# Wider rings and paired tail sums in the gather layers of a four-layer GNN kernel

## The reference

```python
edge_index = stack([src, dst])
# layer 0: tanh((segment_sum(sigmoid(att) * x[dst], src)) @ W0.T + b0)
# layer 1: h = where(deg > 0, segment_sum(x[src], dst), x);  h @ W1.T + b1
# layer 2: segment_sum(x[src] * edge_weight, dst)
# layer 3: segment_sum(x[src] * (edge_weight_n2 * edge_weight), dst)
x = layernorm(x + layer(x, ...))        # four times
```

## Time and profile before

| | |
|---|---|
| time, median of 3 runs | 11979.11 us (11966.0 to 11984.94) |
| the profiled execution's own time | 11878.79 us |
| its span | 11877.0 us |
| busy: PE, PEld, DVE, ACT, POOL | 8897.3, 5666.5, 7726.7, 5860.3, 8022.3 us |
| indirect gathers L801 | 5175, 4910.8 us busy |
| scatter stage and start | to 3946 us |
| gather layers 0, 1, 2 | 3946 to 6485, 6572 to 9178, 9228 to 11827 us |

### The profile page before, as it was taken

One profiled execution on the slowest core, in us unless ns is written; L12 is line 12 of the kernel. 1 busy time (PEld: TensorE's weight loads), 2 busy tenths in 40 slices (PEclk: granted clock), 3 DMA queues, 4 the chain that ended last, 5 costly groups with the idle time before them and its releaser, 6 DMA issues. The chain is left out here.

```text
span 11877.0 us, 171360 instructions
## 1 busy us (share of the span) xinstructions
PE 8897.3 (75%) x49605; PEld 5666.5 (48%) x49606; DVE 7726.7 (65%) x19171; ACT 5860.3 (49%) x13187; POOL 8022.3 (68%) x7169
## 2 busy tenths in 40 slices
PE   4787888888886455566666787888887788888887
PEld 2444444444444234444546455454445455554445
DVE  8777777777774655544444776666665776666665
ACT  4766555555553444333332665544443766544443
POOL 5787788888887566666665566666665566666665
PEclk8877777777776676767777899989988899889998
DMA  5433333334334211111111111111111111111111
GB/s 145 47 38 35 36 37 38 39 38 38 38 38 70 51 25 25 25 25 24 24 24 27 27 24 25 25 25 24 25 24 28 28 25 25 25 25 25 23 24 30
DMA packets 651932, 398.90 MB, mean 34 GB/s; under 512 B 456994, under 2 KB 563748, under 8 KB 649745
## 3 DMA queue, kind: packets, MB, share of 16 engines
q0 software_dynamic: 445920, 252.47, 17.5%
q1 hardware_dynamic: 201276, 132.08, 4.3%
q10 hardware_dynamic: 3814, 3.37, 0.1%
HBM read 283.23 MB, written 104.16 MB: 33 GB/s over the span
## 5 line engine op out<-in xcount | busy, mean ns | idle before, releaser
L801 POOL DMA_INDIRECT mem<-xt,mem x5175 | 4910.8, 949 | 2864.1 <-issue 1338.3
L1148 PE MATMUL ps<-mem 128*128 128x392 f32 (+5 forms) x6750 | 2905.2, 536 | 1079.8 <-DVE mem L1708 448.9
L722 POOL DMA_INDIRECT table<-mem,idx x1925 | 3000.4, 1559 | 746.4 <-issue 556.7
L1708 DVE TENSOR_TENSOR mem<-mem,ps 128x392 f32 (+3 forms) x3300 | 1917.4, 581 | 1966.8 <-remote 1007.5
L943 ACT ACTIVATE mem<-iota_f,mem 128x128 f32<-128x128 f32 x4200 | 1319.3, 390 | 2659.8 <-remote 1312.7
L1160 PE MATMUL ps<-mem,xs 128*64 128x94 f32 (+1 forms) x17640 | 2068.5, 271 | 382.5 <-issue 363.2
L1160 PEld LDWEIGHTS ps<-mem,xs 128*64 128x64 f32 (+1 forms) x17640 | 1803.8, 156 | 1026.7 <-issue 979.8
L1689 DVE TENSOR_SCALAR mem<-ps,mem 128x392 f32<-128x392 int16 (+5 forms) x4050 | 2175.9, 556 | 0.0
L1148 PEld LDWEIGHTS ps<-mem 128*128 128x128 f32 (+1 forms) x6750 | 1106.1, 184 | 1936.5 <-issue 1312.5
L922 ACT COPY mem<-zero_c 128x658 f32<-128x658 f32 x1260 | 895.6, 732 | 1370.5 <-remote 896.1
L1181 PE MATMUL ps<-mem 128*64 128x64 f32 (+1 forms) x10350 | 1031.7, 245 | 478.4 <-issue 456.2
(11 more groups left out here) (180 smaller groups left out, 7819.2 us busy)
## 6 DMA issues: line engine op xcount, KB each, us to landing
mem<-xt,mem POOLq DMA_INDIRECT x5175
mem<-key_rows SPq DMA_DIRECT2D x385, 160.0 KB
table<-mem,idx POOLq DMA_INDIRECT x1925
table<-mem POOLq DMA_DIRECT2D x3, 6304.0 KB
mem<-table SPq DMA_DIRECT2D x42, 448.0 KB, 5.2
xt<-xs SPq DMA_DIRECT2D x9, 896.0 KB
mem<-in_x_dram SPq DMA_DIRECT2D x415, 16.0 KB
w_d<-mem SPq DMA_DIRECT2D x2, 1562.5 KB, 7.8
```

The source lines that it names most:

```text
L722: pool.indirect_dma_start(out=tables[i % NTAB][:, :], out_offset=bass.IndirectOffsetOnAxis(ap=idx[:, i % (IDXS * GC):i % (IDXS * GC) + 1], ...
L801: pool.indirect_dma_start(out=gbuf[:, o:o + F], out_offset=None, in_=xt[l][:, :], in_offset=bass.IndirectOffsetOnAxis(ap=src_q[q % 2].bitc ...
L1148: last = pe.matmul(ps_d[b % PSD][:, 0:w], lo_l[:, r * P:(r + 1) * P], blk_l[:, r * DT:r * DT + w], start=(k == 0), stop=(k == parts - 1))
L1708: v.tensor_tensor(at, at, new, ALU.add).then_inc(d_add[l], 1)
```

## The change

The ring of gathered rows grows from six to eight slots, and the ring of tail one-hots from three to four. The product of a tail slot goes to one of four places in two PSUM banks, two slots to a bank. DVE no longer adds a slot's product in the next slot: in each odd slot n it adds those of n - 3 and n - 2, after one wait for both. PE waits for adds in even slots only. The tail one-hots are made one slot ahead and not two. The flush add comes one slot later than before (`ZONE_END[max(n - 1, 0)]` in place of `ZONE_END[n]`). The list pieces shrink to 100 chunks and 23 slots, which gives room for the rings; arrays behind them move up.

```diff
--- before.py
+++ after.py
@@ -54,8 +54,8 @@
 WC = 94
 FAR = 65536.0
 NOWHERE = 1048576.0
-R = 6
-OHR = 3
+R = 8
+OHR = 4
 BR = 10
 PSD = 4
 FZ = 14
@@ -165,7 +165,7 @@
     [max(0.17 * k * d, 0.12 * k * d + 0.14 * d + 0.2) for (_, k), d in zip(BLOCKS, ROWS_OF)], 1.5)
 
 
-QD, QT = 170, 45
+QD, QT = 100, 23
 NQD, NQT = -(-CD // QD), -(-NT // QT)
 
 
@@ -280,10 +280,10 @@
         GW = GC * XW
         gbuf = arena[:, 0:R * GW]
         OW = GC * WD
-        ohr = arena[:, 1950:1950 + OHR * OW]
-        blk = arena[:, 2910:2910 + BR * DT]
-        los = arena[:, 7810:7810 + BR * P]
-        lo_d = arena[:, 9090:9090 + GC * P]
+        ohr = arena[:, 2600:2600 + OHR * OW]
+        blk = arena[:, 3880:3880 + BR * DT]
+        los = arena[:, 8780:8780 + BR * P]
+        lo_d = arena[:, 10060:10060 + GC * P]
 
 
         own = [arena[:, 2910 + p * BT_ * XW:2910 + (p + 1) * BT_ * XW] for p in range(2)]
@@ -381,7 +381,7 @@
         ps_s = [ps[:, (5 + p) * BK:(6 + p) * BK] for p in range(2)]
         ps_d = [ps[:, k * BK:k * BK + DT] for k in range(PSD)]
         ps_d2 = [ps[:, 2 * p * BK:2 * (p + 1) * BK].rearrange("p (h c) -> p h c", h=2)[:, :, 0:DX // 2] for p in range(2)]
-        ps_w = [ps[:, (4 + p) * BK:(4 + p) * BK + WD] for p in range(2)]
+        ps_w = [ps[:, (4 + p) * BK + i * WD:(4 + p) * BK + (i + 1) * WD] for p in range(2) for i in range(2)]
         ps_f = ps[:, 6 * BK:6 * BK + WC]
         ps_x = ps[:, 6 * BK + 2 * P:6 * BK + 3 * P]
         iota_pairs = ps[:, 7 * BK:7 * BK + DT // 2].bitcast(I32)
@@ -1173,12 +1173,12 @@
                             zi += 1
                     pe.wait_ge(gath[n % R], gathered(l, n))
                     pe.wait_ge(oh_done[l], n + 1)
-                    if n >= 2:
-                        pe.wait_ge(acc_add[l], n - 1)
+                    if n >= 4 and n % 2 == 0:
+                        pe.wait_ge(acc_add[l], n - 2)
                     for k in range(GC):
                         o = (n % R) * GW + k * XW
                         q = (n % OHR) * OW + k * WD
-                        last = pe.matmul(ps_w[n % 2][0:M, :], gbuf[:, o:o + M], ohr[:, q:q + WD], start=(k == 0),
+                        last = pe.matmul(ps_w[n % 4][0:M, :], gbuf[:, o:o + M], ohr[:, q:q + WD], start=(k == 0),
                                          stop=(k == GC - 1), skip_group_check=True)
                     last.then_inc(agg_done[l], 1)
                 fixup(l, M)
@@ -1719,8 +1719,8 @@
                         v.wait_ge(acc_add[l], n)
                     if flushed:
                         v.wait_ge(f_add[l], flushed)
-                    v.wait_ge(agg_done[l], n + 1)
-                    v.tensor_tensor(at, at, ps_w[n % 2][0:M, :], ALU.add).then_inc(acc_add[l], 1)
+                    v.wait_ge(agg_done[l], min(n // 2 * 2 + 2, NT))
+                    v.tensor_tensor(at, at, ps_w[n % 4][0:M, :], ALU.add).then_inc(acc_add[l], 1)
 
                 def hots_up_to(b, added):
 
@@ -1731,27 +1731,29 @@
 
                 v.wait_ge(acc_zero, acc_cleared(l))
                 tail_hots(0)
-                tail_hots(1)
+                hot = hots_up_to(0, 0)
                 tail_weights(0)
-                hot = hots_up_to(0, 0)
-                tail_weights(1)
+                flushed = added = 0
                 for n in range(NT):
-                    if n:
-                        tail_add(n - 1, ZONE_END[n - 1] // FZ)
-                    if n + 2 < NT:
-                        tail_hots(n + 2)
+                    if n >= 3 and n % 2:
+                        for m in (n - 3, n - 2):
+                            tail_add(m, flushed)
+                        added = n - 1
+                    if n + 1 < NT:
+                        tail_hots(n + 1)
                     hot = hots_up_to(hot, BLOCK_END[n])
-                    if n + 2 < NT:
-                        tail_weights(n + 2)
-                    if n:
-                        for s_ in range(ZONE_END[n - 1] // FZ, ZONE_END[n] // FZ):
-                            flush_add(s_, n)
+                    if n + 1 < NT:
+                        tail_weights(n + 1)
+                    for s_ in range(flushed, ZONE_END[max(n - 1, 0)] // FZ):
+                        flush_add(s_, added)
+                        flushed += 1
                     for b in range(BLOCK_END[n], BLOCK_END[n + 1]):
                         block_add(b)
                         hot = hots_up_to(hot, b + 1)
-                for s_ in range(ZONE_END[NT - 1] // FZ, NSEG):
-                    flush_add(s_, NT - 1)
-                tail_add(NT - 1, NSEG)
+                for s_ in range(flushed, NSEG):
+                    flush_add(s_, added)
+                for n in range(added, NT):
+                    tail_add(n, NSEG)
                 v.wait_ge(acc_add[l], NT)
                 v.sem_inc(fix_free, 1)
                 fixup(l, M)
```

More of the change, by code:

```diff
@@ L365, in program @@
         nkt = key_f[:, 0:C0]
-        DENSE_AT = 9730
+        DENSE_AT = 10700
         dense = [mem[:, DENSE_AT + p * WC * T:DENSE_AT + (p + 1) * WC * T] for p in range(2)]
```

## The result

The changed kernel took 12043.39 us (median of 4, 12029.55 to 12050.64) where the kernel before took 11980.12 us (11966.0 to 11984.94): a ratio of 1.0059, 95% interval 1.0048 to 1.0071. It is slower by 63 us. The forecast was 11960 us, faster by 19 us; the time is inside the forecast range of 11720 to 12110 us, but on the other side of no change.

The account below looks back on a forecast made before the run. PE's signals were taken to be held back while POOL issues gathers, a beat of about 7.4 us a slot. Terms 0 - 19 - 6 + 10 = -15 us from 11979 gave 11964, stated as 11960 us; range 11720 to 12110.

Parts of the forecast that it names:

- the beat holds: Gather layers: the time per slot follows gathers issued and stays; 11960 us (11900 to 12010), chance 0.50.
- Eight slots: Ring of gathered rows: PE held off longer at layer starts, given back at layer ends; 0, bound +37.5 us.
- Longer runs: POOL's gathers: more runs two slots long between stops; at most 114 us, a sixth taken, -19 us.
- Tail adds: DVE's paired, later adds: the wait moves to block adds at L1708; -6 us, between 0 and -514 us.
- Flush add one slot later: Segment seams: PE's next segment may wait for DVE's later add; +10 us, between 0 and 244 us.
- the seams rival: PE stands at a segment's first zone for the late flush add; 122 us, 12100; chance 0.22, 0.20 of it slower.
- One-hots, smaller pieces: One-hots one slot ahead still come in time, and more list loads on SP delay nobody; 0 each.
- nothing comes faster: Steady part of a layer: POOL waits eight products back, but PE lies two slots further back; 0.

Follow-up runs that it names:

- free condition: Sessions in which the unchanged kernel before took 10666 to 10672 us; the changed kernel measured 0.9982 of it there.
- held condition: Sessions in which the unchanged kernel before took 11885 to 11980 us and POOL stopped in most slots; the changed kernel first measured 1.0059 of it there.
- the session with copies: Kernel before and changed kernel, each with SP copying two times 1 KB HBM to HBM per slot: 12016.37 and 12056.06 us; without copies the kernel before took 11968.72 us.
- four copies: Kernel before and changed kernel, each with SP copying four times 1 KB HBM to HBM per slot: 12093.66 and 12135.88 us.

## Why the prediction was wrong

The case that I forecast was that the beat holds, and where kernels can be compared at one level it did. The forecast said 19 us faster, 63 us slower was measured. The sum failed at the term for the ring; the gain from longer runs wasn't there; the term for the flush add was perhaps too small. From the sum's -15 us to +63 us are 78 us: 27 at the ring, 19 and 6 for two gains that weren't there, and 26 that stay open.

**Eight slots: 0, with +37.5 us as the bound.** This is the step that failed first. I wrote that the stop for the last zones "comes with one slot left and not three. That gives the two slots back: 0". The stop does come with one slot left, 5.97 us long like the 6.00 us of the earlier trace rows. But it gives little back, since what POOL waits for is not what ends the layer: PE has two more slots behind it, and the last zones too. The runs show +27 us for the ring alone, and the trace 6.8, 9.6 and 8.7 us of it at the ends of the three layers. That is 70% of the bound that I had worked out and set aside. In the free condition, where PE has no backlog, the cost is absent.

**Longer runs: -19 us.** Not there. In the session of the ring alone POOL's waits for PE come to 991.9 us ("remote") and 506.6 us (L1181), 1498.5 us in all, where the trace before has 995.1 + 487.0 = 1482.1 us. The ring adds slots to the first run only; the steady stops stay. The term rested on a stop that grows with the run before it, and the very rows that I used speak against that: in the earlier trace rows a single slot lies between 3994.52 and 4003.10 us, 8.58 us, and its stop is 2.63 us, longer than the 2.34 us after two slots. The first eight slots together take (4003.10 - 3946.82) / 8 = 7.04 us each and not the 6.81 us of the first seven. With the ring of eight the stop after one slot is even 6.15 us.

**Tail adds: -6 us, 0 to -514.** The wait moved to L1708 as written: 2707.9 us before L1708 in the changed kernel with the early flush add, against 1966.8, and its tail adds wait for about 180 us. POOL's waits for PE in that kernel are 926.1 + 559.5 = 1485.6 us, again as before. Adds in pairs and later one-hots together are worth nothing that these runs can tell: 1.0022 with them, 1.0024 without them, in two held sessions in which the kernel before is 6 us apart. The pairs with a ring of six never met the held condition.

**Flush add one slot later: +10 us, 0 to +244.** Perhaps too small; by how much, if at all, is not settled. What PE waited for ahead of the zones in the changed kernel has this line (us, times, longest):

```profile
PE ps L1160 <- DVE acc L1714: 55.4, 14, 6.8
```

With the flush add early it is gone; all that stands there is

```profile
  issue: 1329.8, 1969
  DVE mem L1708: 33.0, 39
  DVE mem L1669: 2.3, 2
  DVE mem L1689: 1.7, 3
```

and in the kernel with the ring alone there is no L1714 either. So the mechanism of the seams rival is in the trace; its price is not shown. In time, the whole change lost 63 us in one held session, and all of it but the late flush add lost 25 us in another, which leaves 38 us; by the session with copies it is 40 - 25 = 15 us. But the two losses of the whole change, 63 and 40 us, differ by 23 us themselves, and the changed kernel and its early form were never held in the same session. Against a high price stands the session with copies: there the changed kernel waits for flush adds just as long,

```profile
  DVE acc L1727: 57.7, 15
```

(L1727 is L1714), and what its span gains beyond PE's growing lag behind POOL is 31.6 - 22 = some 9 us, while POOL's waits are the same. (With four copies PE waits 27.5 us for flush adds, and the time lost is 42 us against 40.) So the late flush add costs somewhere between nearly nothing and 38 us, an unsettled part of the rival's 122 us. In the free session the two kernels were the same within 4 us: I take it that DVE's add there comes in time because no signal that DVE waits for is late.

**One-hots, smaller pieces: 0.** Pieces and places: 0.9997 in the free condition. Alone they were not timed in the held one; there they are part of the ring's +27 us.

So of the 63 us the ring carries some 27 and pairs and one-hots nothing that shows; the other 36 us stay open between the late flush add and what one held session has more than another.

**What set the chances wrong.** I read the even beat as tied to gathers issued, through PE's signals. The beat didn't change with the ring or the pairs, which fits. But PE's signals are not held for as long as POOL issues: in the trace before, DVE gets one at 5380.11 us, in the midst of the five gathers begun at 5375.67 us,

```profile
5380.11 0.59 DVE L1708 TENSOR_TENSOR mem<-mem,ps 128x392 f32 x1 [2.23 <-PE ps L1148]
```

and the same five gathers in the free condition leave PE's signals prompt, and 32 more updates a slot hardly slow the held one. So gathers are not by themselves what holds the signals; why the signals are late in one condition is open. Slower had a chance of 0.26, of which 0.20 for the seams; the ring, which by itself makes the kernel slower here, had no rival and no chance of its own. And the rule that "nothing comes faster" from a deeper ring is wrong in the free condition, where the bound is POOL's issue and any stop that a slot of slack removes is won. The rows of the prediction are of the held condition, and that the first result fell in it too was chance. Had it fallen in the free one, the change would have been 20 us faster, almost exactly the 19 us forecast, and that would have been luck: the gain there comes from the ring, which the sum had at 0.

**Which version is best** depends on the condition: the ring of eight with the old order of adds has the lowest median free (10640.89 us beside the changed kernel's 10645.75 us, 5 us, about what a session can tell), the kernel before the lowest held.

## What to carry to other kernels

A deeper ring ahead of a consumer that runs behind moves the producer's lead, not the end: ask what the consumer still has to do when the producer issues its last piece, and count the added slots there (here 25 to 27 us of a bound of 37.5); where the consumer has no backlog they cost nothing. When a wait is taken away from one instruction, look for the next one on the same engine that needs the same signal; here the waits ahead of the tail adds fell by 845 us and those ahead of the block adds rose by 879 us. When a difference of 0.5% is to be split into parts, trace both kernels in the same session. Before two traces are compared, compare each with the median of its own kernel: of 151 us between these, some 90 were the session.

## What the runs showed of the hardware

The same kernel on the same chip took 10666 us in one session and 11885 us in another, each within 0.4% over 14 to 27 runs; all of the difference is in the gather layers, 2157 against 2539 us in the first; the stage ahead of them takes the same time at the same granted clock (0.72 and 0.73 of full speed in the stretch shown). In the free condition PE's mean granted clock there is 0.78 and 0.98 of full speed, in the held one 0.72 and 0.90; PE's busy time for the same instructions is 1336 against 1504 us, less than half of the difference, and PE is not full in either. A PE product reached DVE 0.24 us after its recorded end in one and about 6 us in the other. ACT's and DVE's busy times in that layer agree within 1.3%. Whether the lower clock in the gather layers is a cause of the longer time or follows from PE's waits, and what makes a session the one or the other, no run shows.

The Trainium skill (DMA: Bandwidth & Descriptors, the sections on the anatomy of one DMA on the SWDGE path and on why a DMA increments its semaphore by 16) gives about 100 ns to a semaphore update and 16 updates to a gather; if the 80 of a slot queued, a slot could not take less than an estimated 8.0 us. It takes 6.25 us in the free condition, under 79 ns for each, and in the held one 32 more cost 0.046 us a slot and 64 more 0.12 us, 1.4 and 1.9 ns for each. So at these rates they don't queue one behind another at 100 ns each where PE's signals pass.
